# Cross attention and a 4-bit feed-forward in one Trainium2 kernel: order of x's preparation, first weights and stores of right factors in the t phase

## The chip, the cores and the metric

One core of a Trainium2 chip. The metric is the device time of one launch in microseconds, as the median of several runs. The kernel before takes 604.84 us (three runs, 603.67 to 605.78).

## The reference, cut to what matters

```
# x, ctx: (8, 256, 1024) f32; Wq, Wk: (1024, 1024)
n = layernorm(x)
Q, K = n @ Wq.T + bq, ctx @ Wk.T + bk
x = x + softmax(Q @ K.T / sqrt(1024)) @ ctx
zeros = unpack4(qzeros) + 1                   # per group and column
w = where(unpack4(qweight) > 0, 1, -1)        # 1024 x 1024
W = scales[g_idx] * (w - zeros[g_idx])
out = x + layernorm(x) @ W + bias
```

## The kernel before, in words

Each product is made of three float32r matmuls: a "hi" and a "lo" part of each operand, without lo x lo. Scores are computed as t times ctx, with t = n(x) (Wq.T Wk), so the first phase multiplies the two projections into m (m_hi, m_lo). Then comes the **t phase**, in which the change lies: for 4 pairs p of batches and 8 column blocks j, step n = 8p + j. In each step TensorE sums one group of 24 matmuls (L1253 to L1269), which ScalarE evicts into t_pair (L693). The group of step n waits for the eviction of group n - 4 (L1258), and for xT_lo in its i-th block if j = 0.

In the same steps the other engines do two more jobs, in the order in which the code is written, each engine's queue strictly in that order:

- **x of the next pair.** SP loads x of a batch into xin (load_raw), VectorE takes statistics (x_stats, L835), GpSimd makes rstd (L487), VectorE normalizes (x_apply, L843) and makes dot products with a row (row_terms, L903). SP stores the normalized x to HBM (store_xn, L373) and reads it back in quadrants, four transfers (load_quadrants, L377); VectorE transposes them in blocks of 32 (x_blocks, L856), and in step j = 7 ScalarE and VectorE split them to xT_hi and xT_lo (x_hi L589, x_lo L861). xin has one buffer for raw x, so the load of the next batch waits for x_apply.
- **Right factors of the feed-forward.** The product in the second layer is made of 7 products of half matrices by sums of blocks. For each of four k, weights come from two gathers: VectorE makes a onehot and unpacks (pick, L921), TensorE gathers zeros and scales in two halves (L1225 to L1234), after the groups of steps g and g + 1, where g is the key in GATHER; VectorE makes the weights from each half (L934), one step after it. The second half of a gather waits for the weights of the first (L1232). right_sums (L942) makes four sums; each of the 7 blocks of a k is split, hi on ScalarE (right_hi, L664), lo on VectorE (right_lo, L952), and stored by SP (store_right, L347). There are two part_hi buffers, so right_hi waits for the store of two blocks before.

GATHER (L263) and SUMS (L264) say in which step gathers and sums are; HI_AT and LO_AT (L272 to L275) place two splits in each step from SUMS on. In SP's loop (L390 to L409) x's transfers are written ahead of the stores of right factors of the same step. In VectorE's loop (L965 on) a step does: weights, x_lo (j = 7), pick, right_sums, right_lo, then x's work.

```
GATHER = {2: 0, 4: 1, 8: 2, 10: 3, 15: 4, 17: 5, 21: 6, 23: 7}
SUMS = (6, 12, 19, 25)
# TensorE, after the group of step n
for h in range(2):
    if n - h in GATHER:
        gather(GATHER[n - h], h)
```

In ScalarE's loop (L675 on) a step does: x_hi (j = 7), right_hi, then the eviction of its group.

Of the kernel before, what the change touches and what calls it, by code (L numbers as in the profile page):

```python
# [48 lines left out]
def xattn_ffn_kernel(nc, x, ctx, Wq, bq, Wk, bk, qweight, qzeros, scales, bias, g_idx, out):  # L49
    B, S, D = x.shape  # L50
# [7 lines left out]
    PAIRS = B // 2  # L58
# [11 lines left out]
    with ExitStack() as stack:  # L70
# [173 lines left out]
        def by_quadrant(rows):  # L244

            return rows.rearrange("q (a k i) -> q k a i", a=4, k=NB)
# [13 lines left out]

        block = stack.enter_context(nc.Block())

        GATHER = {2: 0, 4: 1, 8: 2, 10: 3, 15: 4, 17: 5, 21: 6, 23: 7}  # L263
        SUMS = (6, 12, 19, 25)  # L264

        def nibble(i):
            return i // 2 + KH * (i % 2)
# [16 lines left out]
        def _(sp):  # L284
# [41 lines left out]
            def load_ctx(b):  # L326
                if b < 2:
                    sp.wait_ge(s_xlo, NB * PAIRS)
                    if b == 1:
                        for name in R_SUM:  # L330
                            sp.wait_ge(s_lst[name], 16 * KH)
                elif b == 2:
                    sp.wait_ge(s_t, NB * PAIRS)
                else:
                    sp.wait_ge(s_cnlo, 4 * (b - 2))
                    sp.wait_ge(s_ctr, 4 * (b - 2))
                sp.dma_start(cin[b % 3], ctx_rows[b]).then_inc(s_cl[b % 3], 16)
# [9 lines left out]
            def store_right(k, i, low):  # L347
                n, g = RIGHT.index(SPLIT_ORDER[i]), N_PROD * k + i
                if low:
                    sp.wait_ge(s_rlo, g + 1)  # L350
                    name = SPLIT_ORDER[i]
                    sp.dma_start(r_dram[k][:, 2 * n + 1, :], part_lo[k][name].bitcast(F32)).then_inc(s_lst[name], 16)
                else:
                    sp.wait_ge(s_rhi, g + 1)
                    sp.dma_start(r_dram[k][:, 2 * n, :], part_hi[g % 2].bitcast(F32)).then_inc(s_hst[g % 2], 16)
# [9 lines left out]
            def load_raw(b):  # L365
                if b == 2:
                    sp.wait_ge(s_xtr, NB)
                    sp.wait_ge(s_dot, 1)
                else:
                    sp.wait_ge(s_xn, QT * b)  # L370
                sp.dma_start(xin[:, 0, :, :], x_rows[b]).then_inc(s_xraw, 16)

            def store_xn(b):  # L373
                sp.wait_ge(s_xn, QT * (b + 1))
                sp.dma_start(xn_dram[b].rearrange("(t p) f -> p t f", p=P), xin[:, 1, :, :]).then_inc(s_xst, 16)

            def load_quadrants(b):  # L377
                sp.wait_ge(s_xst, 16 * (b - 1))
                if b == B - 2:
                    sp.wait_ge(s_xn, QT * B)  # L380
                if b == B - 1:
                    sp.wait_ge(s_dot, B)
                rows = xn_dram[b].rearrange("(m j) f -> j m f", j=32)
                for a in range(4):
                    sp.dma_start(xq[b // 2][32 * a:32 * a + 32, b % 2 * NB:(b % 2 + 1) * NB, :],
                                 rows[:, :, a * S:(a + 1) * S]).then_inc(s_xql[b % 2], 16)
# [3 lines left out]
            for p in range(PAIRS):  # L390
                for j in range(NB):
                    n = NB * p + j
                    if p < PAIRS - 1:
                        if j in (2, 4):
                            store_xn(2 * p + 1 + j // 2)
                            if 2 * p + 2 + j // 2 < B:
                                load_raw(2 * p + 2 + j // 2)
                        if j == 3 and p < PAIRS - 2:
                            load_quadrants(2 * p + 2)
                        if j == 5:  # L400
                            if p == PAIRS - 2:
                                load_quadrants(2 * p + 2)
                            load_quadrants(2 * p + 3)
                    if n == NB * (PAIRS - 1) + 1:
                        load_ctx(0)
                    for k, i in HI_AT.get(n, ()):
                        store_right(k, i, False)
                    for k, i in LO_AT.get(n, ()):
                        store_right(k, i, True)  # L409
            load_ctx(1)  # L410


# [353 lines left out]
        def _(dve):  # L766
# [68 lines left out]
            def x_stats(b):  # L835
                if b < 2:
                    dve.wait_ge(s_xl[b], 16)
                    ln_stats(xin[:, b, :, :])
                else:
                    dve.wait_ge(s_xraw, 16 * (b - 1))  # L840
                    ln_stats(xin[:, 0, :, :])

            def x_apply(b):  # L843
                dve.wait_ge(s_rstd, b + 1)
                if b == 2:
                    dve.wait_ge(s_xtr, NB)
                elif b > 2:
                    dve.wait_ge(s_xst, 16 * (b - 2))
                for t in range(QT):
                    if b < 2:  # L850
                        out_, in_ = xin[:, b, t, :], xin[:, b, t, :]
                    else:
                        out_, in_ = by_quadrant(xin[:, 1, t, :]), xin[:, 0, t, :].rearrange("q (k a i) -> q k a i", k=NB, a=4)
                    dve.tensor_scalar(out_, in_, mv[:, t, 0:1], rstd[:, t:t + 1], ALU.subtract, ALU.mult).then_inc(s_xn, 1)  # L854

            def x_blocks(b):  # L856
                dve.wait_ge(s_xql[b % 2], 64 * (b // 2))
                tile = xq[b // 2][:, b % 2 * NB:(b % 2 + 1) * NB, :].rearrange("p m f -> p (m f)")
                dve.transpose(tile, tile).then_inc(s_xT, 1)  # L859
# [43 lines left out]
            def row_terms(b):  # L903
                if b == 0:
                    dve.wait_ge(s_wrow, 2)
                dve.wait_ge(s_xn, QT * (b + 1))
                for t in range(QT):
                    for h in range(2):
                        cols = slice(h * HALF, (h + 1) * HALF)
                        i = QT * b + t  # L910
                        order.link(dve.tensor_tensor_reduce(junk, xin[:, min(b, 1), t, cols], (wrow if b < 2 else wrow_q)[:, cols],
                                                            1.0, 0.0, ALU.mult, ALU.add, cdot[:, h, i:i + 1]))
                cols = slice(QT * b, QT * (b + 1))
                order.link(dve.scalar_tensor_tensor(out=ccur[:, cols], in0=cdot[:, 0, cols], scalar=bsum[:, 1:2],
                                                    in1=cdot[:, 1, cols], op0=ALU.add, op1=ALU.add))
                order.link(dve.tensor_scalar(ccur[:, cols], ccur[:, cols], SCALE, None, ALU.mult))
                dve.sem_inc(s_dot, 1)
# [47 lines left out]
            for p in range(PAIRS):  # L965
                for j in range(NB):
                    n = NB * p + j
                    for h in range(2):
                        if n - 1 - h in GATHER:
                            weights(GATHER[n - 1 - h], h)  # L970
                    if j == NB - 1 and p + 1 < PAIRS:
                        for u in range(NB - 2):
                            x_lo(p + 1, u)
                    if n + 1 in GATHER:
                        pick(GATHER[n + 1])
                    if n in SUMS:
                        right_sums(SUMS.index(n))
                    for k, i in LO_AT.get(n, ()):
                        right_lo(k, i)
                    if p < PAIRS - 1:  # L980
                        if j in (1, 3):
                            x_stats(2 * p + 2 + j // 2)
                        if j in (2, 4):
                            x_apply(2 * p + 1 + j // 2)
                            row_terms(2 * p + 1 + j // 2)
                        if j == 5 and p < PAIRS - 2:
                            x_blocks(2 * p + 2)
                        if j == 6:
                            if p == PAIRS - 2:
                                x_blocks(2 * p + 2)  # L990
                            x_blocks(2 * p + 3)
                    elif j == 6:
                        c_lo(0, 0)
                        c_lo(0, 1)
                if p < PAIRS - 1:
                    x_lo(p + 1, NB - 2)
                    x_lo(p + 1, NB - 1)
# [150 lines left out]
        def _(pe):  # L1148
# [104 lines left out]
            for p in range(PAIRS):  # L1253
                for j in range(NB):
# [17 lines left out]
# [3 lines that stand above are left out]
                    if p == PAIRS - 1 and j in (5, 7):  # L1275
# [136 lines left out]
```

## Time and profile before

| | |
|---|---|
| median of three runs | 604.84 us |
| profiled execution | 605.41 us |
| its span, first to last instruction | 603.6 us |
| mean granted TensorE clock | 0.977 of full |
| TensorE busy | 572.3 us, 95% |
| VectorE busy | 388.7 us, 64% |
| ScalarE busy | 215.6 us, 36% |
| HBM traffic | 94.02 MB, mean 156 GB/s |

The t phase runs from about 106 to 322 us of the span. Busy time is a share over the whole span; what matters for the change are the gaps of TensorE in the t phase.

### The profile page before, as it was taken

The numbers are of one execution on the slowest core, as the hardware profiler recorded it, in microseconds if no ns is written. First come the engines' busy times: TensorE is split into PE (matmuls) and PEld (weight loads), VectorE is DVE, ScalarE is ACT, GpSimd is POOL, SyncE is SP. The second block draws the span as 40 slices with busy tenths as digits, with TensorE's granted clock in tenths as the row PEclk, the third lists the DMA queues.
The fourth block names the chain that finished last, engine by engine and source line by source line (L and its number), as shares of the span: only waits on it lengthen the run. The fifth ranks groups of instructions, "written<-read, shape, count | busy, mean of one in ns | idle before, by whom it ended". The sixth has DMA issues, their size and how long they took to land.

```text
span 603.6 us, 7564 instructions
## 1 busy us (share of the span) xinstructions
PE 572.3 (95%) x2798; PEld 471.2 (78%) x2798; DVE 388.7 (64%) x627; ACT 215.6 (36%) x410; POOL 188.0 (31%) x135
## 2 busy tenths in 40 slices
PE   8999999989999679958999999999999999999997
PEld 6788888767777557736889899998778888888886
DVE  4788865579888388837202445476897686767442
ACT  6683444201511241204333766564322231132120
POOL 2062000000000000000033677777576426634630
PEclk9999999989999979987999999999999999999999
DMA  7842100158555925582525489897603303310111
GB/s 242 240 158 72 35 1 1 68 173 229 199 195 143 289 100 174 200 218 105 200 79 199 183 292 363 325 357 305 244 2 139 135 34 110 141 70 1 69 71 70
DMA packets 39028, 94.02 MB, mean 156 GB/s; under 512 B 3096, under 2 KB 17440, under 8 KB 36816
## 3 DMA queue, kind: packets, MB, share of 16 engines
q1 hardware_dynamic: 38992, 93.54, 45.3%
q8 instruction: 22, 0.36, 0.2%
q14 instruction: 14, 0.11, 0.1%
HBM read 59.98 MB, written 33.55 MB: 155 GB/s over the span
## 4 chain that ended last, share of the span: by engine, by line
PE 65%; DVE 14%; DMA 10%; issue 5%; ACT 3%; SPq 2%; POOL 0%; DVEq 0%; ACTq 0%
PE bank L1150 16%; PE bank L1152 16%; PE bank L1151 16%; PE bank L1194 4%; PE bank L1200 4%; PE bank L1197 4%; DMA xin<-in_x 3%; DMA wk_stage<-in_L_xattn_Wk 3%; DVE stats L828 2%; PE bank L1318 2%; PE bank L1250 2%; DMA right_scratch<-part_hi 2%; DVE xin L854 2%; DVE xq L859 1%; DMA xq<-xn_scratch 1%
## 5 line engine op out<-in xcount | busy, mean ns | idle before, releaser
L1150 PE MATMUL bank<-xT_hi,m_hi 128*128 128x512 f32 x256 | 107.4, 420 | 8.3 <-DVE xT_lo L770 8.3
L1152 PE MATMUL bank<-xT_hi,m_lo 128*128 128x512 f32 x256 | 103.4, 404 | 0.0
L1151 PE MATMUL bank<-xT_lo,m_hi 128*128 128x512 f32 x256 | 103.2, 403 | 0.0
L487 POOL TENSOR_TENSOR pairs<-mv,pairs 128x2 f32<-128x2 f32 x16 | 11.7, 733 | 191.5 <-DVE mv L833 191.0
L1104 DVE TENSOR_TENSOR xres<-xres,bank 128x512 f32<-128x512 f32 x56 | 38.4, 686 | 46.2 <-PE bank L1152 46.1
L1150 PEld LDWEIGHTS bank<-xT_hi,m_hi 128*128 128x128 f32 x256 | 49.9, 195 | 22.5 <-issue 8.9
L518 POOL TENSOR_TENSOR l_lo_s<-l_sum_s,l_hi_s 128x512 fp32r<-128x512 f32 x32 | 42.4, 1357 | 71.2 <-DVE l_sum_s L1040 71.2
L504 POOL TENSOR_TENSOR tT_lo<-t_pair,tT_hi 128x1024 fp32r<-128x1024 f32 x16 | 39.2, 2468 | 75.0 <-ACT tT_hi L543 75.0
L693 ACT ACTIVATE t_pair<-bank,ucol 128x512 f32<-128x512 f32 x32 | 21.9, 685 | 111.8 <-PE bank L1152 111.8
L1151 PEld LDWEIGHTS bank<-xT_lo,m_hi 128*128 128x128 f32 x256 | 49.8, 195 | 11.6 <-issue 0.2
L1152 PEld LDWEIGHTS bank<-xT_hi,m_lo 128*128 128x128 f32 x256 | 49.6, 194 | 11.9
L1194 PE MATMUL bank<-wk_hi,wq_hi 128*128 128x512 f32 x128 | 51.3, 401 | 2.5 <-DVE wk_lo L779 2.0
L1197 PE MATMUL bank<-wk_lo,wq_hi 128*128 128x512 f32 x128 | 50.5, 395 | 0.2 <-DVE wk_lo L779 0.2
L1200 PE MATMUL bank<-wk_hi,wq_lo 128*128 128x512 f32 x128 | 50.5, 395 | 0.0
L497 POOL TENSOR_TENSOR cn_lo<-cin,cn_hi 128x512 fp32r<-128x512 f32 x32 | 40.3, 1286 | 27.2 <-ACT cn_hi L543 27.2
L770 DVE TENSOR_TENSOR cT_lo<-bank,cT_hi 128x512 fp32r<-128x512 f32 x32 | 20.6, 685 | 39.5 <-ACT cT_hi L543 39.4
L1150 PE MATMUL bank<-r_tile,l_hi_s 128*128 128x512 f32 x96 | 38.5, 401 | 0.3 <-DVE xres L1104 0.3
L525 POOL TENSOR_TENSOR xres<-xres,bias_rows 128x1024 f32<-128x1024 f32 x16 | 38.0, 2401 | 0.0
L1152 PE MATMUL bank<-r_tile,l_lo_s 128*128 128x512 f32 x96 | 37.8, 394 | 0.0
L1151 PE MATMUL bank<-r_tile,l_hi_s 128*128 128x512 f32 x96 | 37.7, 393 | 0.0
L543 ACT ACTIVATE l_hi_s<-l_sum_s 128x512 fp32r<-128x512 f32 x32 | 20.3, 633 | 48.4 <-DVE l_sum_s L1036 22.5
L1150 PE MATMUL bank<-cT_hi,tT_hi 128*128 128x256 f32 x128 | 36.9, 288 | 0.0
(142 smaller groups left out, 1266.2 us busy)
## 6 DMA issues: line engine op xcount, KB each, us to landing
xin<-in_x SPq DMA_DIRECT2D x8, 1024.0 KB, 7.7
cin<-in_ctx SPq DMA_DIRECT2D x8, 1024.0 KB, 5.7
xres<-in_x SPq DMA_DIRECT2D x8, 1024.0 KB, 11.6
out<-xres SPq DMA_DIRECT2D x15, 512.0 KB, 2.7
right_scratch<-part_hi SPq DMA_DIRECT2D x28, 256.0 KB, 2.3
xn_scratch<-xin SPq DMA_DIRECT2D x6, 1024.0 KB, 4.9
xq<-xn_scratch SPq DMA_DIRECT2D x24, 256.0 KB, 6.2
r_tile<-right_scratch SPq DMA_DIRECT2D x6, 1024.0 KB, 11.4
```

The lines of the kernel that those rows point to most:

```text
L497: pool.tensor_tensor(cn_lo[:, kt, cols], cin[b % 3][:, kt, cols], cn_hi[:, kt, cols].bitcast(F32), ALU.subtract).then_inc(s_cnlo, 1)
L504: pool.tensor_tensor(tT_lo[b][:, ks, :], t_pair[b // 2][:, b % 2, ks, :], tT_hi[b % 2 if b else 2][:, ks, :].bitcast(F32), ALU.subtract).t ...
L518: pool.tensor_tensor(l_lo[name], l_sum[name], l_hi[name].bitcast(F32), ALU.subtract).then_inc(s_llo_p, 1)
L525: pool.tensor_tensor(x1_of(f)[:, t, :], x1_of(f)[:, t, :], bias_rows, ALU.add).then_inc(s_rb, 1)
L693: act.activation(t_pair[p][:, :, j, :], bank[n % 4][:, :].rearrange("p (b q) -> p b q", b=2), ACT.Identity, bias=ucol[:, j:j + 1]).then_in ...
L1104: dve.tensor_tensor(part, part, prod_bank(f, n)[:, :], ALU.add).then_inc(s_acc, 1)
L1150: pe.matmul(out_, a_hi, b_hi, start=start, stop=False, skip_group_check=True)
L1151: pe.matmul(out_, a_hi, b_lo, start=False, stop=False, skip_group_check=True)
L1152: return pe.matmul(out_, a_lo, b_hi, start=False, stop=stop, skip_group_check=True)
L1194: pe.matmul(out_, q_hi, wk_hi[:, c, cols], start=c == 0, stop=False, skip_group_check=True)
L1197: pe.matmul(out_, q_hi, wk_lo[:, c, cols], start=False, stop=False, skip_group_check=True)
L1200: ins = pe.matmul(out_, q_lo, wk_hi[:, c, cols], start=False, stop=c == NB - 1, skip_group_check=True)
```

## The change

The first four gathers (two for each of the first two k) come a step later, and so do the sums and the stores of these two k. x's statistics, normalization and row terms come a step sooner, and x_blocks of a pair's first batch comes in step j = 4 (before: 5; in the last preparing pair it comes in j = 5, before 6). On SP, the stores of right factors stand ahead of x's transfers of the same step; the stores of xn and loads of raw x come a step sooner. The first batch's quadrants are loaded in j = 3 behind both xn stores (j = 4 in the last preparing pair, before 5); before, they stood between the two.

```diff
-        GATHER = {2: 0, 4: 1, 8: 2, 10: 3, 15: 4, 17: 5, 21: 6, 23: 7}
-        SUMS = (6, 12, 19, 25)
+        GATHER = {3: 0, 5: 1, 9: 2, 11: 3, 15: 4, 17: 5, 21: 6, 23: 7}
+        SUMS = (7, 13, 19, 25)
...
                     n = NB * p + j
-                    if p < PAIRS - 1:
-                        if j in (2, 4):
-                            store_xn(2 * p + 1 + j // 2)
-                            if 2 * p + 2 + j // 2 < B:
-                                load_raw(2 * p + 2 + j // 2)
-                        if j == 3 and p < PAIRS - 2:
-                            load_quadrants(2 * p + 2)
-                        if j == 5:
-                            if p == PAIRS - 2:
-                                load_quadrants(2 * p + 2)
-                            load_quadrants(2 * p + 3)
                     if n == NB * (PAIRS - 1) + 1:
                         load_ctx(0)
                     for k, i in HI_AT.get(n, ()):
                         store_right(k, i, False)
                     for k, i in LO_AT.get(n, ()):
                         store_right(k, i, True)
+                    if p < PAIRS - 1:
+                        if j in (1, 3):
+                            store_xn(2 * p + 2 + j // 2)
+                            if 2 * p + 3 + j // 2 < B:
+                                load_raw(2 * p + 3 + j // 2)
+                        if j == (4 if p == PAIRS - 2 else 3):
+                            load_quadrants(2 * p + 2)
+                        if j == 5:
+                            load_quadrants(2 * p + 3)
...
                     if p < PAIRS - 1:
+                        if j in (0, 2):
+                            x_stats(2 * p + 2 + j // 2)
                         if j in (1, 3):
-                            x_stats(2 * p + 2 + j // 2)
-                        if j in (2, 4):
-                            x_apply(2 * p + 1 + j // 2)
-                            row_terms(2 * p + 1 + j // 2)
-                        if j == 5 and p < PAIRS - 2:
+                            x_apply(2 * p + 2 + j // 2)
+                            row_terms(2 * p + 2 + j // 2)
+                        if j == (5 if p == PAIRS - 2 else 4):
                             x_blocks(2 * p + 2)
                         if j == 6:
-                            if p == PAIRS - 2:
-                                x_blocks(2 * p + 2)
                             x_blocks(2 * p + 3)
```

## Rows read from the trace of the kernel before

**Rows 1.** The page: span of the profiled execution.
```profile
span 603.6 us, 7564 instructions
```
**Rows 2.** Busy time by stretches: span, each engine's busy us (instructions), PEclk, DMA share, GB/s.
```profile
210.00:220.00 10.00, 4.65 (x11) 3.69 (x12) 9.00 (x13) 6.78 (x13) 0.00 (x0) 0.51 0.39 147
```
**Rows 3.** Waits of TensorE, 96 to 325 us: total us, times, longest us.
```profile
PE bank L1233 <- DVE wt L940: 2.9, 1, 2.9
...
PE bank L1233 <- DVE wt L940: 8.7, 1, 8.7
PE bank L1150 <- DVE xT_lo L770: 8.3, 2, 7.4
...
PE bank L1233 <- DVE onehot L926: 1.5, 1, 1.5
```
**Rows 4.** Timeline of TensorE: start us, us, operation, [idle before <- releaser].
```profile
220.48 0.39 PE L1151 MATMUL bank<-xT_lo,m_hi 128*128 128x512 f32 x1
220.70 0.39 PE L1152 MATMUL bank<-xT_hi,m_lo 128*128 128x512 f32 x1
```
**Rows 5.** Timeline of ScalarE: evictions of groups 2, 4, 5, 6, 8, 12, 16, 20, one split, 24.
```profile
122.96 0.69 ACT L693 ACTIVATE t_pair<-bank,ucol 128x512 f32<-128x512 f32 x1 [4.89 <-PE bank L1152]
...
140.79 0.69 ACT L693 ACTIVATE t_pair<-bank,ucol 128x512 f32<-128x512 f32 x1 [11.13 <-PE bank L1152]
146.81 0.69 ACT L693 ACTIVATE t_pair<-bank,ucol 128x512 f32<-128x512 f32 x1 [5.33 <-PE bank L1152]
...
152.83 0.69 ACT L693 ACTIVATE t_pair<-bank,ucol 128x512 f32<-128x512 f32 x1 [4.29 <-PE bank L1152]
...
165.09 0.69 ACT L693 ACTIVATE t_pair<-bank,ucol 128x512 f32<-128x512 f32 x1 [1.61 <-PE bank L1152]
...
189.18 0.69 ACT L693 ACTIVATE t_pair<-bank,ucol 128x512 f32<-128x512 f32 x1 [4.29 <-PE bank L1152]
...
223.23 0.69 ACT L693 ACTIVATE t_pair<-bank,ucol 128x512 f32<-128x512 f32 x1 [4.01 <-PE bank L1152]
...
246.87 0.69 ACT L693 ACTIVATE t_pair<-bank,ucol 128x512 f32<-128x512 f32 x1 [2.82 <-PE bank L1152]
...
265.88 0.63 ACT L543 ACTIVATE part_hi<-part_t 128x512 fp32r<-128x512 f32 x1 [11.01 <-DMA right_scratch<-part_hi]
...
281.51 0.69 ACT L693 ACTIVATE t_pair<-bank,ucol 128x512 f32<-128x512 f32 x1 [4.93 <-PE bank L1152]
```
**Rows 6.** Timeline of VectorE: x_apply, row_terms, weights, pick, statistics, right_sums, right_lo, x_blocks.
```profile
125.24 1.54 DVE L854 TENSOR_SCALAR xin<-xin,mv,pairs 128x1024 f32<-128x1024 f32 x2 [0.80 <-POOL pairs L487]
126.81 0.69 DVE L911 CUSTOM_DVE_ANT_0 junk<-xin,uacc 128x512 f32<-128x512 f32 x1
...
130.32 0.69 DVE L938 SCALAR_TENSOR_TENSOR wt<-wt,bank 128x512 f32<-128x512 int32 x1 [0.15 <-DVE ccur L916]
131.05 0.69 DVE L940 TENSOR_TENSOR wt<-wt,bank 128x512 f32<-128x512 f32 x1
...
131.90 0.68 DVE L931 TENSOR_SCALAR wt<-packed 128x1024 int32<-128x1024 int32 x1
135.05 2.47 DVE L828 BATCH_NORM_STATS2 stats<-xin 128x6 f32<-128x512 f32 x4 [2.47 <-DMA xin<-in_x]
...
149.31 0.69 DVE L950 TENSOR_TENSOR part_t<-wt 128x512 f32<-128x512 f32 x1
...
152.04 1.29 DVE L770 TENSOR_TENSOR part_lo_b<-wt,part_hi 128x512 fp32r<-128x512 f32 x2
153.85 2.31 DVE L859 STREAM_TRANSPOSE xq<-xq 128x2048 f32<-128x2048 f32 x1 [0.52 <-DMA xq<-xn_scratch]
```
**Rows 7.** The chain that ended last, its transfers: start us, us until landed, what.
```profile
116.55 4.78 DMA xin<-in_x
...
127.23 7.73 DMA xin<-in_x
...
140.83 4.65 DMA xn_scratch<-xin
...
193.19 8.23 DMA right_scratch<-part_hi
```

## The prediction, made before the changed kernel was built

> **What bounds the kernel now.** I read the span first [rows 1]: TensorE is the bound, so the question is where it stands still while t is summed, and who ends each stop. The chain of waits by engine gives four stops in the t phase [rows 3]: 2.9 us for the first gather's second half (weights not made), 8.3 us in two pieces for xT_lo, of which 7.4 us fall between t groups 15 and 16, 1.5 us for a onehot just before that, and 8.7 us for weights at the end of group 23. Warm matmuls start 0.23 us apart [rows 4], so a group of 24 costs 24 x 0.232 = 5.57 us, and one half of a gather adds 0.45, as the distance of two evictions shows (146.81 - 140.79 = 6.02) [rows 5].
>
> The evictions of t give the whole loss, clock included [rows 5]. From group 2 to 4: 140.79 - 122.96 = 17.8 against 12.0, lost 5.8. From 6 to 8: 12.3 against 11.2, lost 1.1. From 12 to 16 (four groups, one half gather): 34.0 against 22.8, lost 11.3. From 20 to 24 (three half gathers): 34.6 against 23.6, lost 11.0. Together 29.2 us. The losses exceed the waits by 2.9, 2.4 and 2.3 us at the long stops; that is the granted clock, 0.51 in the ten microseconds after the stop at group 16, so the 1.2 GHz level for a while [rows 2]. I charge 2.4 for each long stop.
>
> Behind the two long stops stands one pattern: a store of part_hi is issued on SP behind x's transfers and lands late (8.23 us after issue) [rows 7], ScalarE waits with the next part_hi (11.0 us before 265.88) [rows 5], and VectorE's right_lo, x_blocks and weights queue behind that.
>
> **What the change does to each queue.** No instruction is added or removed. Prices on VectorE, all from [rows 6]: x_apply starts 0.80 behind its statistics (3.0 us long by 2.48 and two small ones) and takes 1.5; row_terms 3.5 (126.81 to 130.32); one half of weights 1.45 (130.32 to 131.75); a pick 0.95; right_sums 2.7 (149.31 to 152.04); two right_lo 1.3; x_blocks 2.3. Transfers: raw x lands 7.7 us after issue when xn's store is issued with it, 4.8 alone; xn 4.65 [rows 7]. Groups of transfers are not in the trace in the new order, so I bound them. A store issued behind xn and raw (2.25 MB in all) lands in 8.2 us, 3.7 per MB; xn, raw and one x of quadrants (3 MB) took from 140.83 to 153.85, 13.0 us, 4.3 per MB [rows 6, 7]. I take 4.1, that is 12.3 for 3 MB; ends: 10.0 (3.3 per MB) and 13.0.
>
> **Pair 0.** The half weights(0,0) moves from VectorE's step 3 to step 4, a step behind x_apply(3) and row_terms(3), which move to step 3. Those wait for raw x 3, and that load can't start before x_apply(2) frees the buffer: it is issued at 127.23 and its statistics start at 135.05, as now [rows 6, 7]. Statistics end 138.0, apply 138.85 to 140.4, row_terms to 143.8, weights(0,0) to 145.3. TensorE is at its wait for them (second half of gather 0) already at 136.5: it reaches gather 0 at 128.5, waits until 130.5 for the onehot, now behind row_terms(2) (2.0 us), and does group 4. So it stands 8.7 us, plus 2.4 of clock. Then x_blocks(2) at step 4 is behind a transfer that SP now issues behind xn 3 and raw 4: 140.4 + 12.3 = 152.7, done 155.0, and weights(0,1) ends 156.4, where TensorE asked at 153.7 (145.3 + 0.45 + 5.57 + 2.4): 2.7 us. At the change of pairs right_sums and two right_lo stand ahead of x_lo(1,6): about 0.7 us. Pair 0 then loses 2.0 + 8.7 + 2.4 + 2.7 + 0.7 = 16.5 against 5.8 + 1.1 now: **+9.6 us**. Ends: raw 3 lands in 4.8 and the quadrants 2.3 earlier, +4.3; two more dips of the clock, +12.
>
> **Pair 1.** Good: the stores of right factors no longer wait behind x. Bad, by walking VectorE from about 173.5: x_stats(5) waits for raw 5 to about 189.5, so weights(2,0), (2,1) and (3,0) come 0.4, 1.5 and 0.4 us late for TensorE. x_apply(5) ends at T = 195.4. From T: xn 5, raw 6 and quadrants of 4 land T + 12.3, x_blocks(4) 2.3, weights 1.4, right_sums 2.7, two right_lo 1.3. Only then, because the low stores are now ahead of it on SP and wait for right_lo, does SP issue the quadrants of x 5: 0.5 + 1.8 of issue, some 4.5 to land (1 MB at 4.1, a bit more for the receipt), x_blocks(5) 2.3, x_hi and x_lo 1.3: T + 30.4. TensorE gets weights(3,0) at T + 5.0, does groups 13 to 15 and two half gathers (17.6), and is there at T + 22.6: it stands 7.8, and 2.4 of clock. Loss 0.4 + 1.5 + 0.4 + 7.8 + 2.4 = 12.5 against 11.3: **+1.2 us**. Ends: with 10.0 and 3 for the two transfers and no short waits -7; with 13 and 8, +5.
>
> **Pair 2.** weights(5,0) 0.4 late; raw 7 lands near 249.5; then statistics 3.0, weights(5,1) 1.4, right_sums and right_lo 4.0 now stand ahead of x_apply(7), done at 259.5, with row_terms 263. right_lo(2,2) and (2,3) end near 265; their stores stand ahead of the quadrants of 6, issued to 267.4, landed near 272.3 (two low stores and one x, 1.5 MB at 4.1, from 266); x_blocks(6) and weights(6,0) end 276. TensorE wants weights(6,0) after group 22, at 269.5 in this walk: 6.5, and 2.4 of clock. The wait at group 23 goes, since x_blocks(7) and weights(6,1) are done within the next group. Loss 0.4 + 6.5 + 2.4 = 9.3 against 11.0: **-1.7 us**. Ends: -10.6 (only the 0.4 left) and +2. From group 24 on the order of before returns and has no stop; I put zero there.
>
> Sum: 9.6 + 1.2 - 1.7 = **+9.1 us**. The profiled execution took 605.41 (1.8 us outside its span); it is 0.6 above the median of the three runs, so I add to the median: 604.84 + 9.1 = 613.9.
>
> **Page against row.** The Trainium skill, "DMA: Bandwidth & Descriptors", section Specifications, gives HBM about 358 GB/s per core. By it 3 MB would take 8.8 us rather than 12.3, an estimate from that page. That would take 3.5 us off pair 1 and pair 0's quadrant wait altogether, and the sum would be near +3, half of the way to rival (a), which is priced from rows. This case's rows show 3.7 to 4.3 us per MB, that is 244 to 283 GB/s, in just this mix, so I go by them.
>
> **Rivals.** (a) Transfers land as fast as when alone, since right stores and x's no longer meet: raw x in 4.8 (row), 3 MB in 10. Then pair 0 is +4.3, pair 1 12.5 - 1.5 - 0.8 - 3.8 = 6.4, so -4.9. In pair 2 x_apply(7) comes 2.9 earlier and the quadrants 1.5 to 2, so 1.8 us of waiting remain without a dip of the clock: 2.2 against 11.0, -8.8. Sum -9.4: **595.5**. It decides in favour of faster once raw 7 lands before 247.5 and the wait at weights(6,0) is below about 2 us. For it: 4.78 is in the trace; against: xn's store is always issued with the next raw load, and that pair took 7.7 us. 15%. (b) Pair 0 and 1 as forecast, but pair 2's stop vanishes, because the late VectorE catches up while TensorE stands at group 16: 9.6 + 1.2 - 10.6 = +0.2, **605**. 10%. (c) Every short wait (2.0, 2.7, 1.5 us) also drops the clock, and x 5's quadrants land 3 us later behind right stores: +2.4 x 3 + 3 more, **624**. For it: the 2.9 us wait did drop it. Against: the shorter piece of the wait for xT_lo (0.9 us) [rows 3] cost no more than 1.1 in the evictions, so no dip. 12%.
>
> **Numbers.** Forecast 63%, with 608 to 620 as its own range. Range 601 to 621: it takes in (b) and the near parts of (a) and (c). A measurement tells 0.3% (1.8 us) from no change. Faster (a) and a bit of (b): 0.17. Same: most of (b): 0.08. Slower: 0.75.
>
> **What would show it.** In pair 0 a wait of 8 to 9 us of TensorE on weights ending near 145, and group 8's eviction near 175 instead of 165.1. In pair 1 one wait of 7 to 8 us on xT_lo near 225, with ScalarE no longer held 11 us by a store of part_hi. In pair 2 a wait on weights after group 22, none after 23. The forecast is wrong if weights(0,0) ends before 140, or if the eviction of group 24 lies before 283.

## The result, and the profile after

The changed kernel takes 622.15 us (median of 4 runs, 621.02 to 623.48) against 604.35 for the kernel before: ratio 1.0292, 95% interval 1.026 to 1.0324, so 17.8 us slower. The forecast was 613.9 with 601 to 621: the right sign, half of the size, and just outside the range. The same program run again later took 618.42 (5 runs, 617.39 to 620.83) against 606.15, ratio 1.0207 (1.0185 to 1.0228). The loss is therefore 12 to 18 us; of the 5.5 us between the two, 3.7 come from the changed kernel and 1.8 from the kernel before. Of all executions timed here one stands far out, 1452.53 us, one of the ten of the kernel with x_blocks back in step 5 below, whose nine others took 603.64 to 606.86; nothing here shows what held it.

The page of the changed kernel: span, TensorE, and the granted clock in 40 slices. TensorE's busy time is 3.6 us longer for the same number of matmuls, with a mean granted clock of 0.970 where it was 0.977, and 15.9 us are added to the span.

```profile
span 619.5 us, 7563 instructions
...
PE 575.9 (93%) x2798; PEld 473.9 (76%) x2798; DVE 389.5 (63%) x627; ACT 216.6 (35%) x410; POOL 187.9 (30%) x135
...
PEclk9989999996899977997999999999999999999999
```

Waits of TensorE in the t phase, in total, which answer to [rows 3]. The weights now hold it five times and 18.8 us, where it was twice and 11.6.

```profile
PE bank L1229 <- DVE wt L938: 18.8, 5, 7.8
PE bank L1146 <- DVE xT_lo L768: 11.2, 2, 10.8
PE bank L1229 <- DVE onehot L924: 2.2, 1, 2.2
```

The same waits one by one, from TensorE's timeline:

```profile
133.80 0.38 PE L1229 MATMUL bank<-zz,onehot 72*128 72x512 bf16 x1 [2.23 <-DVE onehot L924]
147.75 0.61 PE L1229 MATMUL bank<-zz,onehot 72*128 72x512 bf16 x1 [7.79 <-DVE wt L938]
...
159.56 0.38 PE L1229 MATMUL bank<-zz,onehot 72*128 72x512 bf16 x1 [2.91 <-DVE wt L938]
...
199.45 0.38 PE L1229 MATMUL bank<-zz,onehot 72*128 72x512 bf16 x1 [1.94 <-DVE wt L938]
...
234.28 0.76 PE L1146 MATMUL bank<-xT_hi,m_hi 128*128 128x512 f32 x1 [10.75 <-DVE xT_lo L768]
...
283.53 0.61 PE L1229 MATMUL bank<-zz,onehot 72*128 72x512 bf16 x1 [6.05 <-DVE wt L938]
```

The evictions of groups 1, 8, 16 and 24 in ScalarE's timeline cut the t phase into its three pairs, as [rows 5] do before. First group 1 in the trace of the kernel before, which those rows lack:

```profile
117.38 0.69 ACT L693 ACTIVATE t_pair<-bank,ucol 128x512 f32<-128x512 f32 x1 [3.78 <-PE bank L1152]
```

Then the changed kernel:

```profile
120.47 0.69 ACT L691 ACTIVATE t_pair<-bank,ucol 128x512 f32<-128x512 f32 x1 [3.78 <-PE bank L1148]
...
179.67 0.69 ACT L691 ACTIVATE t_pair<-bank,ucol 128x512 f32<-128x512 f32 x1 [1.61 <-PE bank L1148]
...
242.30 0.69 ACT L691 ACTIVATE t_pair<-bank,ucol 128x512 f32<-128x512 f32 x1 [3.01 <-PE bank L1148]
...
297.33 0.69 ACT L691 ACTIVATE t_pair<-bank,ucol 128x512 f32<-128x512 f32 x1 [3.00 <-PE bank L1148]
```

Measured in this way, the kernels give the rows of the table below, in microseconds; for those further down the text has the pairs. The stretch from group 24 to 31 is 40.3 in every kernel of this study, so the loss lies ahead of it. The second column is the eviction of group 1, ahead of which no edit changes what TensorE does.

| kernel | group 1 at | pair 0 (1 to 8) | pair 1 (8 to 16) | pair 2 (16 to 24) | median |
|---|---|---|---|---|---|
| before | 117.4 | 47.7 | 58.1 | 58.3 | 604 to 606 |
| changed | 120.5 | 59.2 | 62.6 | 55.0 | 622.2 |
| changed, again | 118.5 | 59.3 | 61.8 | 56.8 | 618.4 |
| stores ahead only | 117.9 | 47.7 | 55.0 | 54.9 | 597.6 |
| gathers later only | 117.0 | 51.8 | 54.1 | 58.6 | 605.7 |
| x sooner only | 117.1 | 62.3 | 56.8 | 55.2 | 614.5 |
| x sooner + stores ahead | 120.8 | 61.7 | 56.9 | 54.5 | 614.2 |
| gathers later + stores ahead | 116.6 | 52.1 | 54.4 | 55.0 | 603.6 |

The three pairs lose 11.5, 4.5 and -3.3 us, 12.7 in all. The other 3.1 us of the profile lie ahead of group 1, where the code is the same: the last wk slice lands later (ScalarE waits 4.44 us for it instead of 2.85), VectorE and TensorE follow, and the granted clock is 0.83 from 30 to 40 us (1.00 before, and 1.00 in the second profile of the changed kernel). Group 1 was evicted between 116.3 and 120.8 in the profiles of this study, without a relation to the edit that I can show. The pairs themselves also vary: pair 0 of the changed kernel took 59.2 and 59.3, and 61.2 and 60.9 in two kernels below whose edit lies in pair 1 alone. A difference of 2 us or less between two single profiles is therefore not a result.

### The profile page after: what moved, and what is told of

Read it like the earlier page. It is cut to its first block, busy times and chain, and to the rows that moved or that the text cites. A ratio compares the mean times of both kernels' runs of the same rounds, so it can differ in the third digit from the quotient of the medians.

```text
span 619.5 us, 7563 instructions
## 1 busy us (share of the span) xinstructions
PE 575.9 (93%) x2798; PEld 473.9 (76%) x2798; DVE 389.5 (63%) x627; ACT 216.6 (35%) x410; POOL 187.9 (30%) x135
## 4 chain that ended last, share of the span: by engine, by line
PE 63%; DVE 16%; DMA 12%; ACT 3%; issue 3%; SPq 2%; POOL 0%; DVEq 0%; ACTq 0%
PE bank L1146 15%; PE bank L1148 15%; PE bank L1147 15%; DMA xq<-xn_scratch 5%; DMA xin<-in_x 4%; PE bank L1190 4%; PE bank L1196 4%; PE bank L1193 4%; DVE stats L826 3%; DMA wk_stage<-in_L_xattn_Wk 3%; PE bank L1314 2%; PE bank L1246 2%; DVE xq L857 1%; DVE xin L852 1%; SPq L385 1%
## 5 line engine op out<-in xcount | busy, mean ns | idle before, releaser
L485 POOL TENSOR_TENSOR pairs<-mv,pairs 128x2 f32<-128x2 f32 x16 | 11.6, 722 | 203.6 <-DVE mv L831 203.1
L1146 PEld LDWEIGHTS bank<-xT_hi,m_hi 128*128 128x128 f32 x256 | 50.1, 196 | 25.6 <-issue 12.3
L495 POOL TENSOR_TENSOR cn_lo<-cin,cn_hi 128x512 fp32r<-128x512 f32 x32 | 40.3, 1291 | 27.3 <-ACT cn_hi L541 27.3
L541 ACT ACTIVATE l_hi_s<-l_sum_s 128x512 fp32r<-128x512 f32 x32 | 20.3, 633 | 48.3 <-DVE l_sum_s L1032 22.4
## 6 DMA issues: line engine op xcount, KB each, us to landing
r_tile<-right_scratch SPq DMA_DIRECT2D x6, 1024.0 KB, 11.5
```

What stands on the lines that cost most here:

```text
L495: pool.tensor_tensor(cn_lo[:, kt, cols], cin[b % 3][:, kt, cols], cn_hi[:, kt, cols].bitcast(F32), ALU.subtract).then_inc(s_cnlo, 1)
L1146: pe.matmul(out_, a_hi, b_hi, start=start, stop=False, skip_group_check=True)
```

## The experiments

**The three parts by themselves.** The first edit moves only SP's order:

```diff
+                    for k, i in HI_AT.get(n, ()):
+                        store_right(k, i, False)
+                    for k, i in LO_AT.get(n, ()):
+                        store_right(k, i, True)
                     if p < PAIRS - 1:
                         if j in (2, 4):
                             store_xn(2 * p + 1 + j // 2)
...
-                    for k, i in HI_AT.get(n, ()):
-                        store_right(k, i, False)
-                    for k, i in LO_AT.get(n, ()):
-                        store_right(k, i, True)
```

> The kernel before with one part of the change alone: on SP the stores of right factors stand ahead of x's transfers of the same step; gathers, sums and VectorE's order as before. Theory 1 (the change loses by what it moves on VectorE, not by SP's order): ScalarE is no longer held 11 us by a store of part_hi in pair 1, the stop at group 16 shrinks from 8.9 us to 3 to 5, pair 0 is unchanged, sum -4 to -8 us, so about 598. Theory 2 (SP's order is what costs, since quadrants now wait for low stores): +5 us or more, with a longer wait for xT_lo at group 16.

Measured: 597.58 against 605.54, ratio 0.9866 (0.9831 to 0.99), 8 us faster. Theory 1 holds. One row of ScalarE's timeline of the kernel before, and then two of this kernel, show what is left of the hold in pair 1: 6.0 us where there were 11.6.

```profile
201.49 0.63 ACT L543 ACTIVATE part_hi<-wt 128x512 fp32r<-128x512 f32 x1 [11.63 <-DMA right_scratch<-part_hi]
```

```profile
190.80 0.63 ACT L543 ACTIVATE part_hi<-wt 128x512 fp32r<-128x512 f32 x1 [0.45 <-DVE part_lo_b L770]
...
201.97 0.63 ACT L543 ACTIVATE part_hi<-part_t 128x512 fp32r<-128x512 f32 x1 [6.04 <-DMA right_scratch<-part_hi]
```

The stop at group 16 shrank from 7.4 (and 1.5 ahead of it) to 6.3 us, less than I expected, and the one at group 23 from 8.7 to 5.7.

The second has GATHER and SUMS of the change and nothing else:

```diff
-        GATHER = {2: 0, 4: 1, 8: 2, 10: 3, 15: 4, 17: 5, 21: 6, 23: 7}
-        SUMS = (6, 12, 19, 25)
+        GATHER = {3: 0, 5: 1, 9: 2, 11: 3, 15: 4, 17: 5, 21: 6, 23: 7}
+        SUMS = (7, 13, 19, 25)
```

> The kernel before with the first four gathers, sums and splits a step later and nothing else. Theory 1 (the cost is weights standing behind x_apply and row_terms of the second batch): here weights(0,0) stands only behind x_stats(3), so the wait at gather 0 ends near 139.4, 4.9 us plus clock: pair 0 +1.5 us; pair 1 within 3 us; sum about +2, 603 to 609. Theory 2 (the later step of the gathers by itself is the loss): +10 us or more.

Measured: 605.74 against 605.54, ratio 1.0013 (0.9992 to 1.0033), no difference. weights(0,0) end at 139.4, as worked out, since they stand behind the statistics that wait for raw x 3:

```profile
135.05 2.47 DVE L828 BATCH_NORM_STATS2 stats<-xin 128x6 f32<-128x512 f32 x4 [4.63 <-DMA xin<-in_x]
...
138.66 0.69 DVE L940 TENSOR_TENSOR wt<-wt,bank 128x512 f32<-128x512 f32 x1
```

Pair 0 loses 4.0 us, where I had expected 1.5: TensorE also waits 2.7 us for xT_lo at group 8. Pair 1 gains 4.0. The later step is not bad in itself: it is bad for the first k and good for the second.

The third has x's work and transfers a step sooner, with x's transfers still ahead of the stores on SP and the old gathers:

> The kernel before with x's work a step sooner on VectorE and SP, x's transfers still ahead of the stores on SP, gathers and sums in their old steps. Theory 1: weights(0,0) stands behind x_stats(3), which waits for raw x 3: the wait at the first gather's second half is about 8 us and pair 0 loses 5 us more than before; pair 1 and 2 keep their store-bound stops; sum +3 to +8. Theory 2 (x sooner is harmless, the gathers do it): within 2 us of before.

Measured: 614.50 against 605.54, ratio 1.0146 (1.0112 to 1.018), 9 us slower. The sign is theory 1's, the size above its +3 to +8; pair 0 loses 14.6 us, three times what I had expected from one wait. There are three: 1.8 for the onehot, 8.4 for weights(0,0) as expected, and one of 5.2 for the next half, which was not in the expectation.

The fourth takes the changed kernel and puts GATHER and SUMS back:

> The changed kernel with GATHER and SUMS as before: x sooner and SP's new order stay. Theory 1: pair 0's wait for weights(0,0) ends at about 142 instead of 147.7 and the wait for weights(0,1) goes too, pair 0 gains 5 to 8 us against the changed kernel; pair 1 gains since right_sums and right_lo no longer stand between x_blocks(4) and the quadrants' issue: 609 to 614 in all. Theory 2 (the step of the gathers doesn't matter): 620 to 623. It also shows whether the first 30 us, unchanged in the code, again start the t phase 3 us late.

Measured: 614.20, ratio 1.0151 (1.0105 to 1.0198), 8 us under the first measurement of the changed kernel and 4 us under the second. The total is 0.2 us above the range, the reason half right: pair 1 is 4.9 to 5.8 us shorter, pair 0 gains nothing (61.7; a wait of 6.3 us for weights(0,1) stays). SP's order, worth 8 us alone, is worth nothing on top of x sooner (614.20 and 614.50). That showed that the parts don't add up, and that something in x's part was unnamed.

**The changed kernel again.**

> The changed kernel once more, unaltered. The profiles so far show the t phase 12.7 us longer and 3.1 us of delay in the first 30 us, which the change doesn't touch. If the early delay is a matter of the single run, this profile may start the t phase near 117 and the median falls to 617 to 620; if it belongs to this program, it starts near 120 again and the median stays near 622. The t phase from the eviction of group 1 to that of group 24 should again be 176 to 178 us.

Measured: 618.42, with group 1 at 118.45 and the t phase at 177.9. So the early delay is not fixed to this program, and the loss in the t phase is 12.7 us in one profile and 13.8 in the other. What differs inside it is taken up in the section on the prediction.

**What holds the weights in pair 0: the row terms?**

```diff
                         if j in (1, 3):
                             x_apply(2 * p + 2 + j // 2)
-                            row_terms(2 * p + 2 + j // 2)
+                        if j in (2, 4):
+                            row_terms(2 * p + 1 + j // 2)
```

> The changed kernel with row_terms a step later than x_apply, as their result is wanted only by the softmax. Theory 1 (pair 0's time is set by the quadrants of x 2, which land near 155.8 and hold weights(0,1), not by the row terms): the first stop gets 3.5 us shorter and the next one as much longer, so pair 0 stays within 1.5 us of 59.2, and the sum within 2 us of the changed kernel. Theory 2 (row terms ahead of the first weights are the loss): 3.5 us or more faster, pair 0 at 55.7 or less.

Measured: 628.57 against 606.15, ratio 1.0371 (1.0356 to 1.0386), the slowest kernel of the study, and neither theory. VectorE's timeline of this kernel tells why:

```profile
134.49 2.47 DVE L826 BATCH_NORM_STATS2 stats<-xin 128x6 f32<-128x512 f32 x4 [6.80 <-DMA xin<-in_x]
...
137.39 0.69 DVE L909 CUSTOM_DVE_ANT_0 junk<-xin,uacc 128x512 f32<-128x512 f32 x1
...
140.96 1.53 DVE L852 TENSOR_SCALAR xin<-xin,mv,pairs 128x1024 f32<-128x1024 f32 x2 [0.22 <-DVE ccur L914]
```

In the changed kernel row_terms(2) ran while VectorE waited for raw x 3 and cost nothing. Placed behind the statistics of step 2, it runs after that wait: the wait grows from 3.2 to 6.8 us, and the 3.5 us now stand ahead of x_apply and of everything that hangs on it. All three pairs are longer than in the second profile of the changed kernel, by 3.1, 3.7 and 3.0 us.

**The place of the last quadrants on SP.** In step 13 they are issued ahead of the stores:

```diff
+                    if p == 1 and j == 5:
+                        load_quadrants(2 * p + 3)
                     for k, i in HI_AT.get(n, ()):
...
-                        if j == 5:
+                        if j == 5 and p != 1:
                             load_quadrants(2 * p + 3)
```

> The changed kernel, but in step 13 SP issues the quadrants of x 5 ahead of that step's stores, not behind them. Theory 1 (the stop at group 16 is set by these quadrants, which wait on SP for right_lo): they land near 215 instead of 230.4, x_blocks(5) then only waits for VectorE's own queue, and the stop of 10.8 us shrinks by 4 to 6: pair 1 at 57 to 59 instead of 62.6. Theory 2 (the stores or VectorE's queue set it, the place on SP is nothing): within 1.5 us.

Measured: 614.92, ratio 1.0149 (1.0131 to 1.0167), 3.5 us under the changed kernel timed beside it. The stop at group 16 falls to 5.84 us, pair 1 takes 57.9. Theory 1 holds: the quadrants' place behind the low stores costs 4.9 us of the stop of 10.75, or 2.9 of the 8.70 in the second profile of the changed kernel. In what is left x_blocks(5) no longer waits for its transfer, so it stands in VectorE's own queue.

**x_blocks back in step 5.** One number of the change is undone, VectorE's step for x_blocks of a pair's first batch:

```diff
-                        if j == (5 if p == PAIRS - 2 else 4):
+                        if j == 5:
                             x_blocks(2 * p + 2)
```

> The changed kernel with x_blocks of a pair's first batch in step 5 in all pairs, so that weights(0,1) is no longer behind it. Theory 1 (short waits each cost clock as well, and x_blocks(2) waiting for its transfer holds the weights): the 2.9 us wait at the second gather and its 1.7 us of clock go, pair 0 at 54.5 to 56 instead of 59.2; pair 1 and 2 unchanged within 1 us. Theory 2 (what the weights leave, x_blocks takes back at the end of the pair): pair 0 unchanged, a longer wait for xT_lo at group 8.

Measured: 605.19 against 606.15, ratio 0.9983 (0.9969 to 0.9998). This one step is worth 13.2 us by median and 13.7 us between the evictions of groups 1 and 24: with it undone the changed kernel is as fast as before. Pair 0 is at 54.1, just under the 54.5 to 56 that I expected, and pair 1 at 53.1, where I had expected no change. First the changed kernel, VectorE's timeline:

```profile
155.80 2.31 DVE L857 STREAM_TRANSPOSE xq<-xq 128x2048 f32<-128x2048 f32 x1 [7.26 <-DMA xq<-xn_scratch]
158.04 0.65 DVE L936 SCALAR_TENSOR_TENSOR wt<-wt,bank 128x512 f32<-128x512 int32 x1
...
214.07 2.31 DVE L857 STREAM_TRANSPOSE xq<-xq 128x2048 f32<-128x2048 f32 x1 [8.36 <-DMA xq<-xn_scratch]
216.30 0.65 DVE L936 SCALAR_TENSOR_TENSOR wt<-wt,bank 128x512 f32<-128x512 int32 x1
...
220.51 1.29 DVE L768 TENSOR_TENSOR part_lo_b<-wt,part_hi 128x512 fp32r<-128x512 f32 x2
...
230.43 2.31 DVE L857 STREAM_TRANSPOSE xq<-xq 128x2048 f32<-128x2048 f32 x1 [5.14 <-DMA xq<-xn_scratch]
```

and SP's, with the low stores, the quadrants of x 5 and the next four stores:

```profile
221.23 0.92 SPq L352 DMA_DIRECT2D right_scratch<-part_lo_b  x2
222.19 1.99 SPq L385 DMA_DIRECT2D xq<-xn_scratch  x4
224.22 0.92 SPq L355 DMA_DIRECT2D right_scratch<-part_hi  x2
225.19 0.60 SPq L352 DMA_DIRECT2D right_scratch<-part_lo_b  x1
225.83 0.79 SPq L352 DMA_DIRECT2D right_scratch<-part_lo_t  x1
```

Then VectorE's timeline with x_blocks in step 5:

```profile
197.10 0.69 DVE L936 SCALAR_TENSOR_TENSOR wt<-wt,bank 128x512 f32<-128x512 int32 x1 [0.70 <-PE bank L1230]
...
201.34 1.29 DVE L768 TENSOR_TENSOR part_lo_b<-wt,part_hi 128x512 fp32r<-128x512 f32 x2
204.78 2.31 DVE L857 STREAM_TRANSPOSE xq<-xq 128x2048 f32<-128x2048 f32 x1 [2.15 <-DMA xq<-xn_scratch]
...
212.30 2.31 DVE L857 STREAM_TRANSPOSE xq<-xq 128x2048 f32<-128x2048 f32 x1 [3.07 <-DMA xq<-xn_scratch]
```

and SP's of the same kernel:

```profile
202.06 0.92 SPq L352 DMA_DIRECT2D right_scratch<-part_lo_b  x2
203.03 1.98 SPq L385 DMA_DIRECT2D xq<-xn_scratch  x4
```

Both wait for the same transfer. In step 4, VectorE stands 8.4 us at x_blocks(4) with weights(3,1), right_sums and right_lo behind it, and SP stands behind right_lo with the quadrants of x 5. In step 5 that work is done during the wait. The quadrants of x 5 go out 11.5 us after x_apply(5) (191.5 to 203.0) and not 21.4 us after (200.8 to 222.2).

Is it one cause or two? The same edit in one pair at a time:

> The changed kernel with x_blocks of the first batch in step 5 in pair 0 only (step 4 stays in pair 1). Theory 1 (two separate costs: in pair 0 the weights behind x_blocks, in pair 1 the low stores and with them the quadrants of x 5 behind x_blocks): pair 0 at 54 to 55, pair 1 stays at 61 to 63, the sum 5 us under the changed kernel in the same job's terms, 613 to 616. Theory 2 (pair 0's delay is what puts pair 1 late): pair 1 falls below 58 as well.

> The changed kernel with x_blocks of the first batch in step 5 in pair 1 only (step 4 stays in pair 0). Theory 1: pair 0 stays at 59 to 60, pair 1 at 53 to 54, the sum 8 to 9 us under the changed kernel, 609 to 612. Theory 2: pair 1 stays at 58 or more.

Measured: in pair 0 only, 613.88 (ratio 1.0142, 1.0112 to 1.0172), pairs at 54.6, 61.4, 56.6. In pair 1 only, 613.92 (1.0135, 1.0096 to 1.0174), pairs at 60.9, 52.8, 56.9. Each pair gains its own part: 4.7 us of 59.3 in pair 0, 9 of 61.8 in pair 1. The other pair does not gain with it: it takes 61.4 for 61.8, and 60.9 for 59.3. Two costs, theory 1. That they add up is shown by the profiles alone: from group 1 to 24 the two edits gain 5.3 and 7.3 us, together 12.6, and both at once 13.7. The medians gain 4.5 and 4.5, which is 4 us less than the 13.2 of both at once, and the second is above its expected 609 to 612. Its group 1 was at 119.0, that of the kernel with both at 116.3.

**Does the step of x_blocks hurt without the later gathers?**

> The kernel before with x's work a step sooner (as x_sooner, which took 9 us more than before), but x_blocks of the first batch again in step 5. Theory 1 (x_blocks(2p+2) in step 4, ahead of weights and waiting for a transfer, is most of the change's loss, whatever the gathers' step and SP's order): pair 0 falls from 62.3 to 55 to 57, the sum lies at 604 to 609. Theory 2 (x_blocks only hurt together with the later gathers and sums): within 3 us of 614.5.

Measured: 612.66, ratio 1.0136 (1.0104 to 1.0168), only 1.8 us under x_sooner and not to be told from it by the ratios. Pair 0 falls from 62.3 to 57.4, near what theory 1 said. Pair 1 stays at 57.8: with x's transfers ahead of the stores ScalarE is held by a store of part_hi there, as before the change. Neither theory as a whole: by the profiles the step costs about 5 us in pair 0 in both kernels in which it was tried, and in pair 1 it costs 9 us in the changed kernel and nothing here. Whether SP's order alone or only together with the sums in step 13 makes the 9 us was not tried.

**Better versions.** Two of the three parts:

> The kernel before with two of the three parts: stores ahead on SP and first gathers, sums a step later; x's work in its old steps. Theory 1 (the parts add up as long as x_blocks is not ahead of weights: pair 0 from the gathers 51.7, pair 1 51 to 53, pair 2 55): 598 to 601. Theory 2 (the later gathers and the stores ahead cost together, through low stores in front of the quadrants of x 5): pair 1 at 58 or more and 604 or more.

Measured: 603.64, ratio 0.9971 (0.9947 to 0.9994), between the two theories' ranges. Pair 0 pays the 4.4 us of the first k's later gather; pair 1 is at 54.4, so the gains of the two parts there (3.1 and 4.0) don't add: both shorten the same stop at group 16, from 7.4 us to 6.3 and 4.6 alone and to 4.6 together. Next, the later step for the second k only:

```diff
-        GATHER = {2: 0, 4: 1, 8: 2, 10: 3, 15: 4, 17: 5, 21: 6, 23: 7}
-        SUMS = (6, 12, 19, 25)
+        GATHER = {2: 0, 4: 1, 9: 2, 11: 3, 15: 4, 17: 5, 21: 6, 23: 7}
+        SUMS = (6, 13, 19, 25)
```

> Stores ahead on SP, and only the second k's gathers and sums a step later (GATHER 2, 4, 9, 11, 15 ..., SUMS 6, 13, 19, 25). Theory 1 (the first k's later gather costs 4 us in pair 0 behind x_stats(3), the second's later gather gains in pair 1): pair 0 47.7, pair 1 51 to 54, pair 2 55, 594 to 597. Theory 2 (no gain in pair 1 beyond SP's order): 597.6 as sp_order within 1.5 us.

Measured: 596.90 against 605.15, ratio 0.9865 (0.9846 to 0.9885), pairs at 46.8, 52.8 and 54.8. It is 8.3 us faster than before and in its expected range. Beside the 597.58 of the stores alone the medians can't tell the two apart; by the profile pair 1 is 2.3 us shorter, with a stop at group 16 of 4.2 us for 6.3, and 3.6 us shorter in the profile of the next kernel, which has this edit too. Last, row_terms a step later, this time ahead of the statistics:

> As sp_second_later, and row_terms of each x a step later, behind weights and ahead of the statistics that wait for raw x. Theory 1 (the stop at gather 0 in pair 0 is row_terms(2) ahead of weights(0,0); behind them it lies in the wait for raw x 3): the 3.4 us wait and its 2.4 us of clock go, pair 0 at 42 to 43, 589 to 592. Theory 2 (raw x 3 or the next work takes it back): pair 0 within 2 us of 47.7.

Measured: 597.39, ratio 0.9873 (0.9847 to 0.99), no gain. Pair 2 takes 58.2 for 54.8, with a stop of 8.4 us at group 23 for 5.4. Pair 0 stays at 48.3, as in theory 2: the wait at the first gather is gone, and TensorE waits at the second instead, for weights(0,1), which stand behind the statistics of raw x 3:

```profile
138.99 0.58 PE L1234 MATMUL bank<-zz,onehot 72*128 72x512 bf16 x1 [4.58 <-DVE wt L940]
```

## Why the prediction was right in sign and wrong in size

The chains of waits that the prediction walked were found, and neither of its signs of being wrong came: weights(0,0) ended at 147.7 and group 24 was evicted at 297.3. Three terms of its sum were too small: the clock in pair 0 (2.4 us for one dip, 5.0 paid), the stop at group 16 in pair 1 (7.8 us, 10.75 measured), and the stretch ahead of group 1, which was put at nothing (3.1 us in the first profile, 1.1 in the second).

- **Pair 0**, forecast loss 16.5, measured 18.4 (59.2 less 40.8 for seven warm groups and four half gathers). The waits came as worked out: onehot 2.23 for 2.0, weights(0,0) 7.79 for 8.7, weights(0,1) 2.91 for 2.7, group 8 0.49 for 0.7; 13.4 for 14.1. The term that failed is the clock: 2.4 us charged once, 5.0 paid, of which 2.9 in the group with the 7.8 us wait and 1.7 in the group with the 2.9 us wait. Rival (c) had this part: the clock had risen to full by 154 us, and after the 2.9 us wait, which ended at 159.6, it fell again, as these stretches of the changed kernel show:

```profile
154.00:156.00 2.00, 2.00 (x10) 1.63 (x9) 0.20 (x1) 0.00 (x0) 0.00 (x0) 1.00 1.13 221
...
160.00:162.00 2.00, 2.00 (x7) 1.61 (x6) 1.78 (x3) 0.00 (x0) 0.00 (x0) 0.63 0.03 8
162.00:164.00 2.00, 2.00 (x6) 1.53 (x5) 1.81 (x1) 0.00 (x0) 0.00 (x0) 0.51 0.00 0
```

  The prediction reads the 0.51 of [rows 2] as the clock after the stop at group 16. That stop of the kernel before lasted from 207.9 to 215.4 us, so half of the row lies inside it; the 2.4 us charged for the dip come from the evictions and don't hang on this.

- **Pair 1**, forecast loss 12.5, measured 15.8. The stop at group 16 was put at 7.8 and took 10.75. The chain was right link by link; two transfers were sized too short. From x_apply(5), xn 5, raw 6 and the quadrants of 4 took 13.3 us (200.8 to 214.07), where I took 12.3, above even my upper end of 13.0. The last quadrants landed 6.7 us after their last issue began, where I took 4.5. In both I counted only x's own transfers. SP's timeline has right stores among them: two of part_hi, issued at 206.9, in the first, and in the second two low stores just ahead of the quadrants and four stores right behind, 1.5 MB beside the 1 MB of quadrants. That this traffic is what took the time is likely but not shown: in pair 0, where the quadrants of x 3 and no stores follow, the first chain took 13.0 us (142.8 to 155.8), and no kernel has it with nothing behind. The chain's transfers in the changed kernel:

```profile
186.76 8.21 DMA xin<-in_x
...
204.44 9.60 DMA xq<-xn_scratch
...
223.73 6.68 DMA xq<-xn_scratch
```

  In the second profile of the same program the stop is 8.70 us, nearer to the forecast, and pair 1 is no more than 0.8 us shorter. There another term failed, which the first profile does not show: behind a wait of 1.97 us for weights(2,1) the clock fell for about 3 us, and group 12's eviction comes 9.7 us after group 11's, which is 6.0, the wait and 1.7 more. Behind the 1.94 us wait of the first profile the clock stayed full (1.00 from 200 to 202 us). TensorE's timeline and a stretch of the second profile:

```profile
197.58 0.38 PE L1229 MATMUL bank<-zz,onehot 72*128 72x512 bf16 x1 [1.97 <-DVE wt L938]
...
200.00:202.00 2.00, 2.00 (x6) 1.63 (x5) 1.90 (x7) 0.00 (x0) 0.00 (x0) 0.50 1.04 362
```

- **Pair 2**, forecast loss 9.3, measured 7.8: the wait at weights(6,0) was 6.05 for 6.5, and the one at group 23 is gone, as forecast.
- Sum in the t phase: +9.1 forecast, +12.7 and +13.8 measured in two profiles. These and the delay ahead of group 1 (3.1 us in one profile, 1.1 in the other) give the span. What sets that delay stays open, and so does the rest of the 3.7 us between the two medians. The forecast of 613.9 missed 622.15 by 8.2 us and 618.42 by 4.5.
- The conclusion I did not draw: my own sum had x_blocks(2p+2) ahead of the weights in pair 0 and ahead of the low stores in pair 1, as two ordinary links among many. Those two places cost as much as the whole change loses: without that one step it is even with the kernel before. It is even by a balance, since pair 0 still takes 54.1 for 47.7, behind the late weights(0,0), and pairs 1 and 2 give 5.0 and 1.3 back.
- Rival (a), transfers landing as fast as alone, is refuted: raw x took 7.0 to 8.2 us in the three pairs, not 4.8. The rate of about 358 GB/s that the Trainium skill gives as HBM's limit for a core in "DMA: Bandwidth & Descriptors", Specifications, would put 3 MB at 8.8 us, an estimate from that page; the run took 13.3. That is 237 GB/s for these 3 MB, and 259 GB/s from 200 to 214 us with the stores among them, so here the measurement decides. Rival (b) is out as well, since the stop in pair 2 stayed. Rival (c), with 624, is the nearest number to 622.15, and partly by luck: of the short waits that it names one dropped the clock in the first profile (2.9 us) and two in the second (3.4 and 1.97 us), never all three, and its 624 has nothing for the 3.1 us ahead of group 1.

## What to carry to other kernels

An operation that waits for a transfer costs what is queued behind it in order, on its own engine and on the queue that waits for that engine. When it is moved, list the work that it is moved ahead of, and ask of each piece who needs it; moving one such operation a step later, behind that work, was worth 13 us here. Work that fills a wait is free only on the near side of the wait: the same row terms behind it made the kernel 10 us slower. And when a change has several parts, time each alone and then in pairs, since the part that gains (the stores ahead, 8 us) can be hidden entirely by another.

## What the runs showed that I had not expected

A wait of 2.9 us of TensorE cost 1.7 us more in clock, soon after another dip. Short waits of nearly the same length cost differently: the 1.94 us ahead of 199.45 next to nothing (group 12's eviction comes 8.1 us after group 11's, which is 6.0 and the wait), the 1.97 us at the same place of the same program's second profile 1.7 us. Quadrants of x, 1 MB read in 1 KB pieces, took 6.7 us from the last issue with six right stores of 256 KB around them (238 GB/s from 223 to 230 us), and 9.6 us behind two transfers of 1 MB. And the first 30 us, which no edit touched, moved the start of the t phase by up to 4.5 us between profiles.
